# A two-layer gated attention and expert kernel: the second layer's down products lag by two periods, and VectorE copies weights with a maximum over one element

## What is computed

```python
x = hidden_states.reshape(-1, H)                    # 2048 tokens, H = 256, already normalized
probs = jax.nn.softmax(x @ router_w, axis=-1)       # E = 32 experts
topk_w, topk_idx = jax.lax.top_k(probs, TOP_K)      # TOP_K = 4 experts per token
topk_w = topk_w / jnp.sum(topk_w, axis=-1, keepdims=True)
combine = jnp.sum(one_hot(topk_idx, E) * topk_w[..., None], axis=1)
g = jnp.einsum('th,ehi->tei', x, w_gate)            # I = 192
u = jnp.einsum('th,ehi->tei', x, w_up)
act = jax.nn.silu(g) * u
eo = jnp.einsum('tei,eih->teh', act, w_down)
routed = jnp.einsum('te,teh->th', combine, eo)
# a shared expert, silu(x @ sh_gate) * (x @ sh_up) @ sh_down times a sigmoid, is added
```

## Time and profile before

| what | before |
|---|---|
| median of three executions | 1312.74 us (1307.31 to 1315.9) |
| the profiled execution, its own time | 1314.94 us |
| span of its trace, first to last instruction | 1313.2 us |
| the 40 periods in question | about 1052 to 1277 us of the span |

### The profile page before, as it was taken

How to read it: one execution, slowest core, us unless ns; L and a number is a source line. 1 busy time by engine, 2 the same in 40 slices (tenths; PEclk the granted TensorE clock), 3 DMA queues, 4 the chain that set the end, 5 groups by cost and what they waited for, 6 DMA issues and landing times. The chain is left out here.

```text
span 1313.2 us, 26054 instructions
## 1 busy us (share of the span) xinstructions
PE 1231.0 (94%) x9183; PEld 931.9 (71%) x9184; DVE 758.4 (58%) x1547; ACT 662.9 (50%) x1471; POOL 694.6 (53%) x686
## 2 busy tenths in 40 slices
PE   4999897999999999999999989999799989999976
PEld 2777656888888888888888876776656645555545
DVE  6787774444444454554444436777569455555544
ACT  2777854544545554554555437666231144444443
POOL 5565305666656555655566453332027747777750
PEclk9999998999999999999999999999789999999998
DMA  7334343444444444444455458000400168887858
GB/s 257 49 58 66 57 145 113 109 104 106 107 104 106 107 104 92 93 94 108 112 112 113 117 117 314 24 6 2 160 3 0 33 190 243 237 236 234 231 142 320
DMA packets 139032, 161.72 MB, mean 123 GB/s; under 512 B 79142, under 2 KB 104364, under 8 KB 137649
## 3 DMA queue, kind: packets, MB, share of 16 engines
q1 hardware_dynamic: 104656, 106.23, 26.6%
q0 software_dynamic: 32256, 52.46, 19.4%
q10 hardware_dynamic: 2016, 1.71, 0.4%
HBM read 122.60 MB, written 39.85 MB: 124 GB/s over the span
## 5 line engine op out<-in xcount | busy, mean ns | idle before, releaser
L1402 POOL DMA_INDIRECT x_dram<-e_y,rows x128 | 217.4, 1699 | 191.0 <-ACT e_y L1511 165.7
L1546 DVE TENSOR_TENSOR e_hid<-e_sg,bank 128x512 f32<-128x512 f32 x128 | 88.1, 688 | 128.3 <-PE bank L1437 94.8
L1498 ACT CAST e_hidden_hi<-e_hid 128x512 fp32r<-128x512 f32 x128 | 79.4, 621 | 161.4 <-DVE e_hid L1546 161.4
L1437 PE MATMUL bank<-e_xg_hi,e_w_hi 128*128 128x512 f32 x512 | 159.0, 392 | 2.0 <-issue 2.0
L1340 POOL DMA_INDIRECT spare<-xn_dram,rows x128 | 124.9, 976 | 64.2 <-issue 38.4
L1437 PE MATMUL bank<-e_xg_hi,e_w_lo 128*128 128x512 f32 x512 | 158.2, 390 | 0.0
L1437 PE MATMUL bank<-e_xg_lo,e_w_hi 128*128 128x512 f32 x512 | 158.1, 390 | 0.0
L1549 DVE TENSOR_TENSOR e_hidden_lo<-e_hid,e_hidden_hi 128x512 fp32r<-128x512 f32 x128 | 88.7, 693 | 87.9 <-ACT e_hidden_hi L1498 87.9
L2102 PE MATMUL bank<-w,e_xT 128*64 128x384 f32 x320 | 111.9, 492 | 2.2 <-DVE e_wt L2207 1.7
L1511 ACT ACTIVATE e_y<-bank,shares 128x256 f32<-128x256 f32 x128 | 60.7, 474 | 105.4 <-PE bank L1450 105.1
L2102 PE MATMUL bank<-e_wt,e_xT 128*64 128x384 f32 x320 | 112.0, 493 | 0.0
(11 more groups left out here) (329 smaller groups left out, 2630.9 us busy)
## 6 DMA issues: line engine op xcount, KB each, us to landing
w<-in_L_ffn_w SPq DMA_DIRECT2D x48, 512.0 KB
kT<-in_L_down SPq DMA_DIRECT2D x108, 192.0 KB
wgu<-in_L_gate_up SPq DMA_DIRECT2D x8, 1536.0 KB, 9.2
V<-in_L_down SPq DMA_DIRECT2D x52, 192.0 KB
kT<-ys_dram SPq DMA_DIRECT2D x4, 1024.0 KB, 8.3
xn_dram<-V SPq DMA_DIRECT2D x5, 512.0 KB, 11.1
X<-in_x SPq DMA_DIRECT2D x4, 512.0 KB, 9.2
b_cT<-in_ctx_p SPq DMA_DIRECT2D x4, 512.0 KB, 11.8
```

Of the source, the lines that this page charges most:

```text
L1402: nc.gpsimd.indirect_dma_start(out=x_dram[:, :], out_offset=bass.IndirectOffsetOnAxis(ap=rows[:, e, q:q + 1], axis=0), in_=y[q][:, :], in_ ...
L1437: last = nc.tensor.matmul(bank[f % 2][:, :], w[:, k * F0 + f * 128:k * F0 + (f + 1) * 128], x[:, k, h * SLOTS:(h + 1) * SLOTS], start=(w, ...
L1498: nc.scalar.copy(hidden[0][:, f, :], hid[f % 2][:, :]).then_inc(hi_sb, 1)
L1546: nc.vector.tensor_tensor(hid[f % 2][:, :], sg[f % 2][:, :], U_BANK[f % 2][:, :], ALU.mult).then_inc(hid_sb, 1)
```

## The change

The order on TensorE becomes `up(t+2)`, `up(t+3)`, `turn_hidden(t)`, `turn_over(t+4)`, `turn_over(t+5)`, `down(t-2)`; the first period has no down product and one more stands behind the last. `take_result` on VectorE moves with it, to tiles t-2 and t-1. `hidT` and its PSUM bank become two each, the ring of down weights grows from 6 to 8 tiles (its fourth pair of places lies in `picked[0]`, the buffer `spare` of the routing stage), and `take_hidden` gets one more wait. VectorE's `take_weights` becomes a reduction by maximum over an axis of one element in place of a copy. GpSimd's program has no line in the diff.

```diff
-    NBUF, NDOWN = 3, 6
+    NBUF, NDOWN = 3, 8
...
-        wd = [[[p[rows, u, 0:3, :] for u in range(2)] for rows in HALVES] for p in picked[1:NDOWN // 2 + 1]]
+        wd = [[[p[rows, u, 0:3, :] for u in range(2)] for rows in HALVES] for p in picked]
...
-        hidT = sb("hidT", [2 * FT, 3, PT])
+        hidT = [sb(f"hidT{v}", [2 * FT, 3, PT]) for v in range(2)]
...
-        XT, GU, HT, Y = r.banks[0:2], r.banks[2:4], r.banks[4], r.banks[6:8]
+        XT, GU, HT, Y = r.banks[0:2], r.banks[2:4], r.banks[4:6], r.banks[6:8]
...
                 if t + 4 < PAIRS:
                     turn_over(t + 4)
                     turn_over(t + 5)
-                down(t)
+                if t >= 2:
+                    down(t - 2)
+            down(PAIRS - 2)
...
             def take_hidden(t):
                 act.wait_ge(ht_ps, t // 2 + 1)
-                nc.scalar.copy(hidT[:, :, :].rearrange("p c t -> p (c t)"), HT[:, 0:3 * PT]).then_inc(ht_sb, 1)
+                if t >= 4:
+                    act.wait_ge(y_ps, t - 2)
+                nc.scalar.copy(hidT[t // 2 % 2][:, :, :].rearrange("p c t -> p (c t)"), HT[t // 2 % 2][:, 0:3 * PT]).then_inc(ht_sb, 1)
...
-                nc.vector.tensor_copy(wt[t % NBUF][1][:, :], wgu[:, bass.ds(e, 1), :].rearrange("p o n -> p (o n)")
-                                      ).then_inc(wt1_sb, 1)
+                nc.vector.tensor_reduce(wt[t % NBUF][1][:, :], wgu[:, bass.ds(e, 1), :].rearrange("p o n -> p n o"),
+                                        AX_X, ALU.max).then_inc(wt1_sb, 1)
...
                     take_weights(t + 4)
                     take_weights(t + 5)
-                take_result(t)
-                take_result(t + 1)
+                if t >= 2:
+                    take_result(t - 2)
+                    take_result(t - 1)
+            take_result(PAIRS - 2)
+            take_result(PAIRS - 1)
```

More of the change, by code:

```diff
@@ L2108, in turn_hidden @@
                 for c in range(3):
-                    last = nc.tensor.transpose(HT[:, c * PT:(c + 1) * PT], hid[t // 2 % 2][:, c, :, :].rearrange("p s n -> p (s n)"),
+                    last = nc.tensor.transpose(HT[t // 2 % 2][:, c * PT:(c + 1) * PT], hid[t // 2 % 2][:, c, :, :].rearrange("p s n -> p (s n)"),
                                                r.ident[:, :])
@@ L2121, in down @@
                         for u in range(2):
-                            last = nc.tensor.matmul(Y[s][half(u), 0:D], hidT[HALVES[s], c, half(u)],
+                            last = nc.tensor.matmul(Y[s][half(u), 0:D], hidT[t // 2 % 2][HALVES[s], c, half(u)],
                                                     wd[t % NDOWN // 2][s][u][:, c, :], start=c == 0, stop=c == 2)
```

## The result

| what | before | after |
|---|---|---|
| median | 1313.03 us (1307.31 to 1315.9, 4 executions) | 1340.85 us (1333.85 to 1347.31, 4 executions) |
| ratio after to before | | 1.0215, 95% interval 1.0172 to 1.0259 |
| span of the profiled execution | 1313.2 us | 1332.1 us |
| of it, from the stage's first `turn_over` to the end | 261.3 us | 291.7 us |

The change makes the kernel slower by 2.1% (interval 1.7 to 2.6%). Executions of one kernel fall into two groups some 9 us apart, by the granted clock at the start of the routing stage, ahead of the change: it was low in the profiled execution before and not in the one after, so the spans differ by 18.9 us and the medians by 27.8.

What follows compares the result with a forecast made beforehand. TensorE was taken as fullest, waiting once a period on ScalarE's `hidT`. After the change a gather ring binds: +2.5 us up to its first wait, +24.1 over 34 periods, +0.9 tail, +27.5 on 1312.7: 1340 us, range 1322 to 1353.

Steps and rivals of the forecast that it cites:

- The new wait: TensorE at `turn_over` waits for an indirect DMA, about 0.7 us a period.
- one ring: Tokens, result, scatter, gather, then tokens of two periods later, through GpSimd's queue; sets the period at 6.22 us.
- The ring's length: From the landing of one gather's tokens to the next: 12.45 us for two periods, 6.22 each.
- The maximum: VectorE's weight reduction takes 954 ns in place of the copy's 563, +0.39 us each.
- Its loop through the up products: Weights ready later on VectorE delay TensorE's up products: a period of at least 5.43 to 5.63 us.
- The start: First two tiles wait for two longer weight reductions in a row: 0.8 us once.
- the clock: Said to be no rival: TensorE's granted clock was 1.00, its busy share staying about the same.
- The tail: From the last `turn_over` to the end of the products: 11.4 us against 10.46 before, +0.9.
- The rivals: Four other outcomes, chances 0.10, 0.03, 0.06 and 0.05: early landings, faster GpSimd, reduction at copy speed, slower reduction or landings.
- Landings did become shorter: Rival: gathers land after 3.1 us or less in place of 4.2, 1313 to 1321 us; chance 0.10.
- GpSimd's gathers lost their long cases: Rival: VectorE's weight copy blocks GpSimd, the true bound; the change gains 10 us, 1302 us; chance 0.03.

Runs made afterwards that it cites:

- gathers_ahead: Changed kernel with the gathers of tiles t+10 and t+11 a period ahead, before the scatters of t and t+1; ratio 1.0035 to the kernel before.
- lag1_early: Kernel before with VectorE's weights by the maximum, the first taken between the two gated products; down products not moved; ratio 1.0033 to the kernel before.
- two_ahead_early: Changed kernel with gathers two periods ahead in GpSimd's queue and first weights taken between the two gated products; ratio 0.9882 to the kernel before.
- ahead_copy: Changed kernel with gathers a period ahead in GpSimd's queue and VectorE's weights by plain copy again; ratio 0.9975 to the kernel before.
- max_only: Kernel before with only VectorE's weight copy replaced by the maximum, down products not moved; ratio 1.0019 to the kernel before.
- lag_copy: Changed kernel with VectorE's weights by plain copy again, so the later down products stand alone; ratio 1.0232 to the kernel before.

## Why the prediction was right

The forecast was +27.5 us; the medians differ by 27.8, and the stage of the profiled executions by 30.4. That the medians come within 0.3 us is in part luck: the interval of the ratio spans 22.6 to 34.0 us. Of the 30.4, 1.7 are a fall of the clock at the start and 1.0 lies in the combination, both of which the forecast lacked; 27.7 are left for what it counted.

- **The new wait.** TensorE waits at `turn_over` for an indirect DMA, and the chain runs through GpSimd and DMA, as foretold. gathers_ahead shows that it is the cause: it leaves lag and maximum in place and changes only the order. The forecast had one ring that makes every period late by some 0.7 us; the trace has two rings in turn, waits in 20 of 32 periods, and the same mean (20.1 us in 32 periods).
- **The ring's length.** Taken over the 31 turns from t = 12 on, the medians from a landing are: tokens turned over 0.48 us (forecast 0.42), copied 0.95 (0.86), result copied 3.52 (3.52), first scatter 4.32 (4.33), second gather 8.25 (8.25), next landing 12.35 (12.45); the period is 6.24 (6.22). Errors inside cancel: tokens were copied 0.09 later and the register load before the first reduction took 0.3 in place of 0.2, the second one nothing, and the last landing took 4.1 in place of 4.2.
- **The maximum**: 948 ns (954), with no price for one output per element. Its loop through the up products, forecast 5.43 to 5.63, is the 5.55 of gathers_ahead. In the changed kernel it is covered by the ring: with the copy the loss is the same.
- **The start**, forecast +0.8, took +2.5 (11.62 us from the first `turn_over` to the first `turn_hidden` in place of 9.15). Two reductions in a row cost 0.8, as gathers_ahead, lag1_early and two_ahead_early show with 9.93 or 9.92. The rest is the clock, which the prediction had ruled out by the row of 1040 to 1060 us; that row shows one execution, in which it stayed at 1.00. In the timeline after, TensorE has idled 2.11 us for the first weights, and its matmuls take 0.85 us for some 3.5 us before they come back to 0.49:

```profile
1043.17 0.66 PE L2102 MATMUL bank<-w,e_xT 128*64 128x384 f32 x1 [2.11 <-DVE e_wt L2211]
...
1043.63 0.85 PE L2102 MATMUL bank<-w,e_xT 128*64 128x384 f32 x1
...
1046.82 0.49 PE L2102 MATMUL bank<-w,e_xT 128*64 128x384 f32 x1
```

This fall is not the change's: after the same wait of 2.11 us gathers_ahead, lag1_early and two_ahead_early show none, and after a wait of 1.72 us, as in the kernel before, ahead_copy shows one (10.84 us).

- **The tail**: from the last `turn_over`'s end (1282.65) to the end of the products (1294.13) 11.5 us, forecast 11.4. The combination behind it took 1.0 us more than before, which was not forecast; in the other runs it lies between 36.7 and 38.0, with no order by kernel.
- **The rivals.** Landings did become shorter beside a lower load on the DMA engines (0.72 in place of 0.80), but only from 4.2 to 4.1, not to 3.1. GpSimd's gathers lost their long cases: none is over 996 ns, and none over 997 in max_only, where the maximum stands alone. That is what the Trainium skill, "SBUF — State Buffer", section "Who interferes with whom", leads one to expect of a reduction in place of a copy. It gave nothing in time here, because GpSimd was not full but waiting: its queue stood behind results.

## What to carry to other kernels

When a step of a pipeline moves back by a period, look for every queue in which its successors stand in front of something that must come early: a gather behind a scatter inherits the scatter's delay, and its lead is what is lost. Add such a ring up from landing to landing and divide it by the periods it spans; here the longest of these quotients set the period. Then move the early work ahead in the queue as far as its buffers allow, before the instructions themselves are tuned.

## What the runs showed of the hardware that was not expected

- The granted clock of TensorE fell to its lower level behind some waits of TensorE (2.11 us in the start shown above; in lag_copy three periods at a mean of 0.81) and stayed there for 3.4 us, so that such a wait costs 1.7 us more than its own length. Other waits were not followed by a fall: not the same 2.11 us at the start of lag1_early and two_ahead_early, not those of up to 1.4 us in the loop of the changed kernel, where the clock was 1.00 throughout, and not the longest of lag_copy, 2.22 us in the period of 8.66 us at 1.00 shown above. What decides between them the runs do not show.
- In the stretch from 940 to 960 us, at the start of the routing stage, the granted clock was 0.50 in the profiled execution before and 0.98 in the one after, with the same program there. Of the twelve traces eight show 0.50, and the stage of the experts starts at 1049 to 1053 us in them; four show 0.90 to 0.98, and it starts at 1040 to 1044. First the kernel before, then the one after:

```profile
940.00:960.00 20.00, 20.00 (x93) 19.48 (x92) 6.95 (x18) 3.62 (x5) 0.00 (x0) 0.50 0.62 245
```

```profile
940.00:960.00 20.00, 20.00 (x111) 14.44 (x110) 14.50 (x76) 8.17 (x13) 2.53 (x2) 0.98 0.59 232
```

- Between the result that releases GpSimd and the start of its indirect DMA lie some 0.8 us (0.79 in the chain shown after the change, 0.81 in most of its 40 pairs of scatters, 0.77 at least); between two indirect DMAs that wait for nothing lie 0.30 us.
